# Mixing, layer norm and feed-forward done for pairs of tiles, spread over four slots, in a windowed-attention transformer kernel

## What is computed

```python
h = shift_token(x)                       # half of the channels from the token before
q, k, v = jnp.split(h @ wqkv, 3, -1)
q = l2norm(q) * qs ; k = l2norm(k) * ksc ; q, k = rotary_xpos(q, k)
o = local_attention(q, k, v)             # own window and the one before
x = x + o @ wo
h = layernorm(shift_token(x)) * lg + lb
a, g = jnp.split(h @ w1 + b1, 2, axis=-1)
x = x + (a * gelu(g)) @ w2 + b2
```

## Time and profile before

| | us |
|---|---|
| median of 3 runs | 4184.54 |
| lowest and highest | 4182.05, 4185.37 |
| profiled execution, device time | 4177.53 |
| its span | 4175.8 |
| PE, DVE, ACT, POOL busy in the span | 3727.0, 2876.0, 2445.6, 2305.8 |

### The profile page before, as it was taken

How to read it: one execution, slowest core, us unless ns; L and a number is a source line. 1 busy time by engine, 2 the same in 40 slices (tenths; PEclk the granted TensorE clock), 3 DMA queues, 4 the chain that set the end, 5 groups by cost and what they waited for, 6 DMA issues and landing times. The chain is left out here.

```text
span 4175.8 us, 100713 instructions
## 1 busy us (share of the span) xinstructions
PE 3727.0 (89%) x40109; PEld 2537.5 (61%) x40109; DVE 2876.0 (69%) x6495; ACT 2445.6 (59%) x5007; POOL 2305.8 (55%) x2225
## 2 busy tenths in 40 slices
PE   7975999997999979999999999999999998758886
PEld 4653555543665646666666666666666666646665
DVE  3346445411665648888888888888888887548885
ACT  2222555523454547777777777777777776437775
POOL 1004000001121248888888888888888886247773
PEclk9996999998999989999999999999999999879998
DMA  0000000000000012112112112112111111120010
GB/s 20 2 8 22 1 1 1 2 27 7 2 2 2 2 56 58 41 41 67 41 41 67 41 42 66 43 41 67 41 41 41 41 41 29 33 68 22 22 24 20
DMA packets 103246, 128.49 MB, mean 31 GB/s; under 512 B 38232, under 2 KB 55680, under 8 KB 101888
## 3 DMA queue, kind: packets, MB, share of 16 engines
q1 hardware_dynamic: 102784, 122.05, 10.9%
HBM read 31.95 MB, written 3.54 MB: 8 GB/s over the span
## 5 line engine op out<-in xcount | busy, mean ns | idle before, releaser
L398 POOL TENSOR_TENSOR t_inv<-t_ssq,half 128x8 f32<-128x8 f32 x448 | 779.6, 1743 | 89.9 <-DVE t_ssq L674 69.7
L449 PE MATMUL t_wa<-t_w_qkv,t_resid 128*128 128x512 f32 x1344 | 695.0, 617 | 57.4 <-DMA t_b<-in_L_ffn_b 54.6
L409 POOL TENSOR_TENSOR t_ra<-t_qn,t_rot 128x512 f32<-128x512 f32 x448 | 569.7, 1272 | 84.6 <-DVE t_qn L681 76.1
L598 ACT ACTIVATE t_p<-t_p 128x384 f32<-128x384 f32 (+1 forms) x448 | 241.0, 538 | 331.4 <-DVE t_p L698 322.4
L707 DVE TENSOR_TENSOR t_ra<-t_ra,t_rb 128x512 f32<-128x512 f32 x448 | 309.5, 713 | 123.6 <-POOL t_rb L411 123.6
L478 PEld LDWEIGHTS t_T<-ident,t_p 128*96 128x96 f32 (+1 forms) x1792 | 191.7, 128 | 312.2 <-ACT t_p L598 280.2
L410 POOL TENSOR_TENSOR t_rb<-t_qn,t_rot 128x256 f32<-128x256 f32 x448 | 367.6, 821 | 0.0
L411 POOL TENSOR_TENSOR t_rb<-t_qn,t_rot 128x256 f32<-128x256 f32 x448 | 333.1, 744 | 0.0
L449 PEld LDWEIGHTS t_wa<-t_w_qkv,t_resid 128*128 128x128 f32 x1344 | 212.5, 192 | 176.5 <-issue 146.8
L672 DVE TENSOR_REDUCE t_ssq<-t_sq 128x8 f32<-128x512 f32 x448 | 304.7, 680 | 13.9 <-ACT t_sq L590 10.4
L486 PE MATMUL t_T<-ident,t_ra 128*128 128x128 f32 x1792 | 269.1, 277 | 42.5 <-ACT t_gg L637 31.9
(11 more groups left out here) (400 smaller groups left out, 8410.1 us busy)
## 6 DMA issues: line engine op xcount, KB each, us to landing
t_v<-t_vn SPq DMA_DIRECT2D x192, 198.0 KB, 2.6
t_v<-t_vn SPq DMA_DIRECT2D x248, 132.0 KB, 2.4
t_v<-t_vn SPq DMA_DIRECT2D x144, 66.0 KB, 1.9
t_w_qkv<-in_L_ffn_Wqkv SPq DMA_DIRECT2D x6, 1536.0 KB
t_v<-t_nothing SPq DMA_DIRECT2D x48, 66.0 KB, 1.9
t_w_o<-in_L_ffn_Wo SPq DMA_DIRECT2D x6, 512.0 KB
f_h<-t_L_ffn_h_w SPq DMA_DIRECT2D x2, 1024.0 KB, 8.0
t_w<-in_L_ffn_W SPq DMA_DIRECT2D x6, 341.0 KB
```

The lines of the kernel that those rows point to most:

```text
L398: pool.tensor_tensor(inv[:, n % 2, r, :], ssq[:, n % 2, r, :], g["half"][:, 0:8], ALU.pow).then_inc(inved.sem, 1)
L409: pool.tensor_tensor(ra[:, n % 2, r], qn[:, r], spread(cos, 1, 8), ALU.mult).then_inc(cosd.sem, 1)
L449: pe.matmul(bank, resid[:, b, lo:lo + P], w_qkv[:, l % 2, at:at + 512], start=True, stop=True).then_inc(wa_up.sem, 1)
```

## The change

`slots()` hands out pairs of tiles. The period of the whole-tile work becomes 2 NG slots: four in the long stage and two in the short one. In the long stage the first of four slots carries `tail` for two tiles, the second `ffn`, the third the new part `drop` (the down product, ahead of the turned outputs), the fourth `last` (the second residual). In the short stage even slots carry `tail` and `last`, odd ones `ffn` and `drop`, the down product behind the turned outputs as before.

Mixing, gate, up and down products take 256 moving columns instead of 128; the transposes of the residual and of the norm, `bn_stats`, `bn_aggr` and the normed tile are done twice in a row; the additions, the power `rstd`, the GELU and its product take both tiles in one instruction. Gate and up are cut into three banks: gate of chunks 0 and 1, up of chunks 0 and 1, and chunk 2 of both (`both2`). In every slot the first half of the weighting now stands before the turn of q and the second half behind it. The copy of the turned outputs goes to a half of a wider `oT`.

```diff
-        part = lambda s, k: (s - k) // NG - 1 if (s - k) % NG == 0 and 0 <= (s - k) // NG - 1 < NT else None
+        part = lambda s, k: (s - k) // (2 * NG) - 1 if (s - k) % (2 * NG) == 0 and 0 <= (s - k) // (2 * NG) - 1 < NU else None
         group = lambda n: n if 0 <= n < TG else None
         for s in range(-2, TG + NG + 2):
-            yield group(s), group(s + 1), group(s + 2), part(s, 0), part(s, 1), part(s, 2)
+            yield group(s), group(s + 1), group(s + 2), part(s, 0), part(s, 1), part(s, NG), part(s, NG + 1)
...
-        for kind, n in (("p0", now), ("p1", now), ("gate", ffn), ("up", ffn), ("q", turn), ("k", turn), ("o", now)):
+        for kind, n in (("p0", now), ("p1", now), ("gate01", ffn), ("up01", ffn), ("both2", ffn), ("q", turn), ("k", turn), ("o", now)):
...
-        oT = st.sb("oT", [P, NG, 4, P])
...
+        oT = st.sb("oT", [P, NG, 4, 2, P])
...
-        gg = st.sb("gg", [P, NH, P])
-        hT = st.sb("hT", [P, NH, P])
+        gg = st.sb("gg", [P, NH, W])
+        hT = st.sb("hT", [P, NH, W])
...
-        yT, sh2, lnP, fT = (misc[:, i * P:(i + 1) * P] for i in range(4))
+
+        yT = lnP = misc[:, 0:W]
+        sh2 = fT = misc[:, W:2 * W]
...
-                        if was == "gate":
-                            pe.wait_ge(gelu_in.sem, gelu_in.at(m, NH))
-                        elif was == "up":
-                            pe.wait_ge(h_in.sem, h_in.at(m, NH))
+                        if was == "gate01":
+                            pe.wait_ge(gelu_in.sem, gelu_in.at(m, 2))
+                        elif was in ("up01", "both2"):
+                            pe.wait_ge(h_in.sem, h_in.at(m, 2 if was == "up01" else NH))
...
-                def mix_heads(t):
-                    l = layer_of(t)
-                    pe.wait_ge(T_in.sem, T_in.at(copied["o", t * NG + NG - 1]))
-
-                    if NG == 1 and t >= 1:
-                        pe.wait_ge(lnT_in.sem, lnT_in.at(t - 1))
-                    if NG > 1 and t:
-                        pe.wait_ge(tile_done.sem, tile_done.at(t - 1, 2))
+                def mix_heads(u):
+                    l = layer_of(2 * u)
+                    pe.wait_ge(T_in.sem, T_in.at(copied["o", 2 * u * NG + 2 * NG - 1]))
+
+                    if u:
+                        pe.wait_ge(tile_done.sem, tile_done.at(u - 1, 2))
                     for c in range(4 * NG):
-                        m = pe.matmul(yT, w_o[:, l % 2, c, :], oT[:, c // 4, c % 4, :], start=(c == 0), stop=(c == 4 * NG - 1))
+                        m = pe.matmul(yT, w_o[:, l % 2, c, :], oT[:, c // 4, c % 4, :, :].rearrange("p i k -> p (i k)"), start=(c == 0), stop=(c == 4 * NG - 1))
                     m.then_inc(y_up.sem, 1)
...
-                def gate_up(t):
-                    l = layer_of(t)
-                    pe.wait_ge(lnT_in.sem, lnT_in.at(t, 1))
-                    for half, kind in ((1, "gate"), (0, "up")):
-                        bank = turn_bank(kind, t)
-                        for c, (at, size) in enumerate(HC):
+                def turn_residual(u):
+                    b, lo = columns(2 * u)
+                    pe.wait_ge(x1_in.sem, x1_in.at(u, 2))
+                    for i in range(2):
+                        m = pe.transpose(sh2[:, i * P:(i + 1) * P], resid1[:, b, lo + i * P:lo + (i + 1) * P], ident[:, :])
+                    m.then_inc(sh2_up.sem, 1)
+
+                def turn_norm(u):
+
+                    pe.wait_ge(lnd.sem, lnd.at(u, 7))
+                    for i in range(2):
+                        m = pe.transpose(lnP[:, i * P:(i + 1) * P], ln[:, i, :], ident[:, :])
+                    m.then_inc(lnT_up.sem, 1)
+
+                def gate_up(u):
+                    l = layer_of(2 * u)
+                    pe.wait_ge(lnT_in.sem, lnT_in.at(u, 1))
+                    for kind, parts in (("gate01", ((1, 0), (1, 1))), ("up01", ((0, 0), (0, 1))), ("both2", ((1, 2), (0, 2)))):
+                        bank = turn_bank(kind, u)
+                        for i, (half, c) in enumerate(parts):
+                            at, size = HC[c]
                             lo = half * hid + at
-                            m = pe.matmul(bank[0:size, c * P:(c + 1) * P], w_1[:, l % 2, lo:lo + size], lnT[:, :], start=True, stop=True)
+                            m = pe.matmul(bank[0:size, i * W:(i + 1) * W], w_1[:, l % 2, lo:lo + size], lnT[:, :], start=True, stop=True)
                         m.then_inc(T_up.sem, 1)
 
-                def down(t):
...
-                    pe.wait_ge(h_in.sem, h_in.at(t, NH))
-
-                    if NG == 1 and t + 1 < NT:
-                        pe.wait_ge(lnd.sem, lnd.at(t + 1, 4))
+                def down(u):
+                    l = layer_of(2 * u)
+                    pe.wait_ge(h_in.sem, h_in.at(u, NH))
...
                     if ffn is not None:
-                        pe.wait_ge(lnd.sem, lnd.at(ffn, 4))
-                        if NG == 1 and ffn:
-                            pe.wait_ge(tile_done.sem, tile_done.at(ffn - 1, 2))
-                        pe.transpose(lnP, ln[:, ffn % 2, :], ident[:, :]).then_inc(lnT_up.sem, 1)
+                        turn_norm(ffn)
                     if ahead is not None:
                         project("k", ahead)
                     if now is not None:
...
                         mix_heads(tail)
                     if ffn is not None:
                         gate_up(ffn)
-                    if turn is not None and ffn is None:
+                    if now is not None:
+                        weigh(now, 0)
+                    if turn is not None:
                         turn_qk("q", turn)
                     if now is not None:
-                        weigh(now, 0)
                         weigh(now, 1)
-                    if turn is not None and ffn is not None:
-                        turn_qk("q", turn)
                     if tail is not None:
-                        b, lo = columns(tail)
-                        pe.wait_ge(x1_in.sem, x1_in.at(tail, 2))
-                        pe.transpose(sh2, resid1[:, b, lo:lo + P], ident[:, :]).then_inc(sh2_up.sem, 1)
+                        turn_residual(tail)
                     if turn is not None:
                         turn_qk("k", turn)
+                    if drop is not None and NG > 1:
+                        down(drop)
                     if now is not None:
                         turn_o(now)
-                    if ffn is not None:
-                        down(ffn)
+                    if drop is not None and NG == 1:
+                        down(drop)
...
-                            rows, cols = slice(64 * a, 64 * a + 64), slice(lo + a, lo + a + P)
+                            rows, cols = slice(64 * a, 64 * a + 64), slice(lo + a, lo + a + W)
...
-                        v.bn_stats(stats[:, :], sh2).then_inc(lnd.sem, 1)
-                        v.wait_ge(lnd.sem, lnd.at(tail, 1))
-                        v.bn_aggr(mv[:, :], stats[:, :]).then_inc(lnd.sem, 1)
-                        v.wait_ge(lnd.sem, lnd.at(tail, 2))
-                        v.tensor_scalar(vare[:, :], mv[:, 1:2], LN_EPS, None, ALU.add).then_inc(lnd.sem, 1)
+                        for i in range(2):
+                            v.bn_stats(stats[:, i, :], sh2[:, i * P:(i + 1) * P]).then_inc(lnd.sem, 1)
+                        for i in range(2):
+                            v.wait_ge(lnd.sem, lnd.at(tail, i + 1))
+                            v.bn_aggr(mv[:, i, :], stats[:, i, :]).then_inc(lnd.sem, 1)
+                        v.wait_ge(lnd.sem, lnd.at(tail, 4))
+                        v.tensor_scalar(vare[:, :], mv[:, :, 1], LN_EPS, None, ALU.add).then_inc(lnd.sem, 1)
```

69 lines of the change are left out of this document (37 added, 32 removed).

## The result

| | before | after |
|---|---|---|
| median, us (4 runs each) | 4183.3 | 4241.59 |
| lowest and highest | 4181.76, 4185.37 | 4238.6, 4245.85 |
| profiled execution, its span | 4177.53, 4175.8 | 4238.6, 4236.9 |

The changed kernel is 1.4% slower: 1.014 times the kernel before, 95% interval 1.0122 to 1.0157. The prediction was 4228, slower, range 4165 to 4266.

A forecast was written before the change was run, and what follows sets the result against it. The prediction took the chain round PE, POOL and DVE, not one engine's sum, as the bound. Profiled 4177.5 + 53 (long stage) - 9 (short stage) = 4221.5, plus 7.0 to the median: 4228, range 4165 to 4266.

The forecast's parts named there:

- the plain slot: Long-stage slot without whole-tile work: 9.04 us at the start of the stage, the base for the two light slots.
- rival (c): Long stage: down and second residual cost in full, 9.4 and 9.6, GELUs 0.56 each; about 4279, half way 4254; 15%.
- the line through 0.112 and 0.43: PE record times at 128 and 512 columns, 0.83 ns per column between: a 256-column record takes 0.218 us.
- Rival (a): PE products: a 256-column record costs 0.112 us, like 128 columns; four slots 40.2, about 4096 us; 4%.
- Slot 1: Long-stage tail slot for two tiles: maximum, mixing, weighting with turn of q, then normalising, 12.2 us.
- Slot 2: Long-stage feed-forward slot: `both2` waits for two GELUs with weighting, turns and scores queued behind it; 11.9 us.
- Slots 3 and 4: Long-stage slots of the down product and second residual: 9.1 and 9.2 us, bounds 9.04 each and 9.4, 9.6.
- Sum: Four long-stage slots: 42.4 against 41.3 us, 1.1 more per pair; +52 over 47 pairs, long stage +53.
- Changes of layer: Long stage: rotary tables and weight loads given no price; a few us for each of 4 layers if cover is gone.
- Short stage: Two slots there: 12.35 and 12.45, sum 24.8 against 25.42 us; -0.6 for each of some 15 pairs, -9.
- Rival (b): Long stage: fewer switches and earlier half weighting take 0.6 from each heavy slot; four slots 40.9, about 4157 us; 10%.
- (d): Rival of no difference: an error of 0.9 us in the four long-stage slots removes the 1.1 per pair; 9%.

## Why the prediction held

It was right in sign and near in size, 4228 against 4241.59, and right in its mechanism: the light slots stay near the plain slot, and the slots of the tail and of the feed-forward each grow by what stands on PE ahead of DVE's normalising. The rise itself was 58 by the medians, where I had 44. 4241.59 lies half way between my 4228 and the 4254 of rival (c)'s likelier half, so the time alone doesn't tell the two apart; the lengths of the slots do.

- **Width costs in full.** 256 columns take 0.222 us a record, predicted 0.218 from the line through 0.112 and 0.43. Mixing took 3.55 (predicted 3.49), down 1.29 (1.31). Rival (a), width is free, is refuted by these rows, and with it, for these fp32 products, what I had drawn from the Trainium skill (TensorE: Matmul & The Clock Gate, "Back-to-back issue gap"), that a product of 256 columns costs what one of 128 does.
- **Slot 1**: 12.18, predicted 12.2. Point by point: maximum at 1.78 (1.81), mixing 3.54 later (3.54). Two errors cancel, which is luck: weighting with the turn of q between its halves takes 1.82 and not 1.61, and from there to N it is 1.49 in place of 1.37 + 0.4. The second statistics cost 0.21 and not 0.4: from the first of them to N it is 0.82 (2407.05 - 2406.23), where it was 0.61.
- **Slot 2**: 12.30, predicted 11.9. The wait came where it was said, `both2` at 8.78 after N (8.7). The four records took 1.02 where I had 0.87, and weighting and turn 1.82 where I had 1.61: these two terms are the 0.4. The 1.61 was read off rows in which both halves of the weighting lie together; the old order in the paired kernel (0.19 and 0.32 less) and the new one in the unpaired kernel (0.23 more in the tail slot) show the price of splitting them. The unpaired ffn slot's 0.43 and the short stage's 12.71 to 13.23 hold also the wait for the GELU that the second half then stands behind.
- **Slots 3 and 4**: 8.98 and 9.05, predicted 9.1 and 9.2. The cover held better than feared. In slot 4 the maximum does start at 2.37 after N (2.3), and the delay was gone by the end of the slot. Rival (c) is refuted: it had 9.4 and 9.6 here and 0.56 for a GELU of 256 columns, which took 0.41 (two in 0.81).
- **Sum**: 42.50 against 42.4. It is nearer than its parts: slot 2 is 0.4 over, slots 3 and 4 together 0.27 under. 47 pairs cost 55 to 56 where I had 52. Changes of layer cost 3.3 more than before, where I had put no price; which of the tables, the weights' loads or the copy of values behind them it is was not tested. The ends of the stage are what is left, 2 to 3, where I had 1.4.
- **Short stage**: predicted -9, measured -0.8. This is the step that failed by most. The tail slot was 12.43 (12.35), but the ffn slot 12.94 and not 12.45, by the 1.02 of `both2` (0.15 over) and the 1.82 (0.21 over) again, a table load 0.1 later, and 0.13 more from that load to `both2` (2.27, where I had 2.14). About 16 such slots of 0.5 are the missing 8.
- **Together**: own time predicted 4221.5, measured 4238.6. Of the 17 missing, 8 are the long stage, 8 the short one, 1 what lies around them. Rival (b), switches and waits pay, is refuted by slot 2; (d) by the interval.

What the prediction didn't see is how cheap the cure is. It named what is queued behind the waiting product, and moving that product behind it is worth 1.04 per pair, 1.36 with the weighting in one piece.

## What to carry to other kernels

A product that must wait for another engine belongs behind the work that engine doesn't hold up; its place was worth 1.04 us per pair here, nearly the 1.16 that the change lost in the long stage, for a wait of 1.09. Room in a light slot is a sum to be spent once: measure it (here about 0.6 us ahead of the weighting in slot 4, and in slot 3 at least the 0.99 that 8 records of mixing took), cut the moved work to it, and don't count it again for a second edit. When two engines go round each other, a gain in one slot has to be followed into the next: of 0.42 in a tail slot, 0.18 came back as a wait for scores.
